# Projecting two attention heads in one matmul: hi and lo halves summed on VectorE, the division by row sums moved ahead of the output projection, reciprocals spread over partitions by two DMAs

## The reference

```python
q, k, v = (split_heads(layernorm(x) @ W) for W in (Wq, Wk, Wv))   # (B, 16, T, 64)
logits = (q @ k.T + causal + pos_bias) / 64
out = softmax(logits) @ v                    # rows divided by their sum
x = x + layernorm(concat_heads(out) @ Wo + bo)
# then shared FFN + 8 experts, top 2 of them weighted, layernorm, residual
```

## Time and profile before

| what | value |
|---|---|
| median of 3 runs | 843.75 us (843.51 to 843.93) |
| the profiled execution's own time | 844.46 us |
| its span, first to last instruction | 842.7 us |
| mean granted TensorE clock | 0.975 |
| TensorE matmuls busy | 771.5 us (92%) |
| VectorE busy | 707.7 us (84%) |
| ScalarE busy | 612.8 us (73%) |
| GpSimd busy | 298.9 us (35%) |

### The profile page before, as it was taken

The page is one execution under the profiler, slowest core; times in us unless marked ns, Lnnn a source line. Parts: engine busy times, 40 slices in busy tenths (PEclk is TensorE's granted clock), DMA queues, the critical chain, the costliest instruction groups (busy, mean ns, idle before and its releaser), DMA issues.

```text
span 842.7 us, 17198 instructions
## 1 busy us (share of the span) xinstructions
PE 771.5 (92%) x4436; PEld 657.1 (78%) x4436; DVE 707.7 (84%) x1596; ACT 612.8 (73%) x1340; POOL 298.9 (35%) x323
## 2 busy tenths in 40 slices
PE   3877999999999999999999999996489999999992
PEld 2656988888888888888889888885377777777771
DVE  5557888988888888888888888888778888898976
ACT  2356888887888888888788888873577767667672
POOL 2318823333332332333233233223503354445423
PEclk9899999999999999999999999999679999999997
DMA  7684334424423432442443343230003211122101
GB/s 279 219 280 89 75 66 97 88 62 87 100 62 76 95 77 62 93 94 62 87 95 67 70 97 82 62 75 26 25 1 129 76 60 43 46 75 75 51 1 50
DMA packets 56025, 70.72 MB, mean 84 GB/s; under 512 B 36032, under 2 KB 45120, under 8 KB 52544
## 3 DMA queue, kind: packets, MB, share of 16 engines
q1 hardware_dynamic: 55712, 69.83, 32.9%
q10 hardware_dynamic: 288, 0.59, 0.3%
HBM read 27.36 MB, written 9.50 MB: 44 GB/s over the span
## 4 chain that ended last, share of the span: by engine, by line
PE 75%; DVE 8%; issue 6%; POOL 4%; ACT 3%; DMA 3%; POOLq 0%; DVEq 0%; ACTq 0%; SPq 0%
PE out_ps L1191 16%; PE score_ps L1158 16%; PE trans_ps L1173 15%; PE shared_ps L1205 6%; PE trans_ps L1074 3%; PE score_ps L1074 3%; PE score_ps L1076 2%; PE score_ps L1075 2%; PE trans_ps L1075 2%; PE trans_ps L1076 2%; DVE pT_lo L961 2%; PE shared_ps L1074 2%; PE shared_ps L1076 2%; PE shared_ps L1075 2%; POOL rstd L421 1%
## 5 line engine op out<-in xcount | busy, mean ns | idle before, releaser
L649 ACT ACTIVATE probs<-score_ps,row_min 128x128 f32<-128x128 f32 (+7 forms) x256 | 189.9, 742 | 53.5 <-DVE row_min L848 53.4
L861 DVE TENSOR_TENSOR pT_lo<-trans_ps,pT_hi 128x512 fp32r<-128x512 f32 (+3 forms) x384 | 201.6, 552 | 16.7 <-ACT pT_hi L670 16.6
L670 ACT ACTIVATE pT_hi<-trans_ps 128x512 fp32r<-128x512 f32 (+3 forms) x384 | 185.1, 491 | 40.4 <-PE trans_ps L1173 28.8
L848 DVE CUSTOM_DVE_ANT_0 score_ps<-score_ps,bias 128x128 f32<-128x128 f32 (+7 forms) x256 | 194.6, 760 | 22.8 <-PE score_ps L1158 19.4
L1173 PE MATMUL trans_ps<-ident,probs 128*128 128x128 f32 x1152 | 190.0, 274 | 3.2 <-DVE pT_lo L861 1.8
L1158 PE MATMUL score_ps<-k_hl,q_hl 128*128 128x512 f32 (+2 forms) x768 | 182.5, 351 | 3.1 <-DMA k_hl<-k_hl 1.6
L470 POOL TENSOR_TENSOR acc<-acc,head_out 128x512 f32<-128x512 f32 x64 | 83.0, 1297 | 245.5 <-DVE head_out L879 245.3
L1173 PEld LDWEIGHTS trans_ps<-ident,probs 128*128 128x128 f32 x1152 | 136.8, 140 | 27.3 <-DVE pT_lo L861 11.9
L1191 PE MATMUL out_ps<-pT_hi,v_hl 128*128 128x512 f32 (+2 forms) x384 | 156.5, 409 | 1.1 <-DVE pT_lo L861 1.1
L961 DVE TENSOR_TENSOR pT_lo<-probs,pT_hi 128x512 fp32r<-128x512 f32 x144 | 133.2, 952 | 25.0 <-ACT pT_hi L728 15.1
L1158 PEld LDWEIGHTS score_ps<-k_hl,q_hl 128*128 128x128 f32 x768 | 134.4, 189 | 23.7 <-DMA k_hl<-k_hl 1.8
(11 more groups left out here) (122 smaller groups left out, 1163.3 us busy)
## 6 DMA issues: line engine op xcount, KB each, us to landing
q_hl<-k_hl SPq DMA_DIRECT2D x64, 256.0 KB, 3.6
k_hl<-k_hl SPq DMA_DIRECT2D x32, 512.0 KB, 4.2
v_scratch<-probs SPq DMA_DIRECT2D x16, 512.0 KB, 4.0
v_raw<-v_scratch SPq DMA_DIRECT2D x32, 256.0 KB, 4.6
bias_all<-gate_scratch SPq DMA_DIRECT2D x8, 1024.0 KB, 4.8
v_raw<-in_Wfc SPq DMA_DIRECT2D x8, 256.0 KB, 4.9
bias<-in_Wproj SPq DMA_DIRECT2D x8, 256.0 KB, 5.3
bias_all<-in_rel_steps SPq DMA_DIRECT2D x1, 1920.0 KB, 12.7
```

What stands on the lines that cost most here:

```text
L649: act.activation(probs[s % 4][:, 0:n], scores_of(s % QB)[:, 0:n], ACT.Exp, bias=row_min[:, s:s + 1], scale=-1.0, accum_out=row_sum[:, s:s ...
L670: act.activation(pT_hi[c][:, CH * g:CH * g + m, q * P:(q + 1) * P], trans_ps[k % 2][:, 0:m * P].rearrange("p (m q) -> p m q", q=P), ACT.Co ...
L848: dve.tensor_tensor_reduce(out=ps, in0=ps, in1=bias_b[b][:, T - n:T], scale=1.0, scalar=3e38, op0=ALU.add, op1=ALU.min, accum_out=row_min[ ...
L861: dve.tensor_tensor(pT_lo[c][dst], trans_ps[k % 2][:, 0:m * P].rearrange("p (m q) -> p m q", q=P), pT_hi[c][dst], ALU.subtract).then_inc(p ...
```

## The change

Heads are taken in pairs. The product with V of an even head is put into partitions 0 to 63 of a tile `o_pair`, that of an odd head into 64 to 127: ScalarE copies the *other* half of `out_ps` across (64 x 512), and VectorE adds the half of `out_ps` that lies in place. When both heads are there, GpSimd multiplies the tile by `inv_all`, the reciprocals of the row sums as rows that are equal over 64 partitions, and one `project_out` per pair (Wo rows of two heads, 128 deep) goes straight into an `add_pair` on VectorE. `Wo2` holds each row once.

The reciprocals lie one per partition (`row_inv`), and are wanted along the free axis. SP carries them: `store_inv` writes 128 x 4 single floats to a DRAM scratch, `load_inv` waits for it to land and reads 512 floats into each of 64 partitions. The reciprocal of rows of part c = 1 is now computed in slot 9 of its batch's eight (slot 1 of the next half-head), that of c = 0 in slot 5. The last pieces of `values` stand in slot 13 instead of 14, so that VectorE's sum can follow in slot 14. The hardware loop's body holds two heads. How q and k are split is the same on both sides. The core of the diff:

```diff
-    PV1 = [11, 11, 11, 12, 13, 13, 14, 14]
-    WO = [11, 15]
+    PV1 = [11, 11, 12, 12, 12, 13, 13, 13]
+    WO = [12, 15]
+    SUM = [10, 14]
+    INV = [5, 9]
+    SUM_SLOT = {QB * b + SUM[c]: (b, c) for b in range(B) for c in range(NC)}
+    INV_SLOT = {QB * b + INV[c]: (b, c) for b in range(B) for c in range(NC)}
...
+    def in_order(engine, iteration):
+        iteration(0, 0, False)
+        with engine.Fori(1, PAIRS) as m:
+            iteration(m * 2 - 1, m, True)
+            iteration(m * 2, m, False)
+        iteration(H - 1, PAIRS, True)
...
+            def store_inv(h, b, c):
+                u = h * (B * NC) + b * NC + c
+                sp.wait_ge(inv_ready, u + 1)
...
+                rows = slice(QB * b + CH * c, QB * b + CH * (c + 1))
+                sp.dma_start(bass.AP(inv_dram.tensor, (b * NC + c) * W, [[1, P], [P, CH]]), row_inv[:, rows],
+                             allow_slow_non_contiguous=True).then_inc(inv_stored, 16)
+            def load_inv(h, b, c, m, odd):
...
+                sp.wait_ge(inv_stored, (h * (B * NC) + b * NC + c) * 16 + 16)
+                sp.dma_start(inv_all[b][c][half_of(odd), :],
+                             bass.AP(inv_dram.tensor, (b * NC + c) * W, [[0, DH], [1, W]])).then_inc(inv_loaded[b][c], 16)
+            def iteration(h, m, odd):
...
                 load_v(h, 1)
+                if not first:
+                    store_inv(h - 1, 1, 1)
+                    load_inv(h - 1, 1, 1, m, not odd)
                 place_q(h, 1)
                 place_k(h, 1)
+                store_inv(h, 0, 0)
+                load_inv(h, 0, 0, m, odd)
                 if not last:
                     sp.wait_ge(v_ready, h * B + 1)
                     load_v(h + 1, 0)
+                store_inv(h, 0, 1)
+                load_inv(h, 0, 1, m, odd)
+                if not last:
                     place_q(h + 1, 0)
                     place_k(h + 1, 0)
+                store_inv(h, 1, 0)
+                load_inv(h, 1, 0, m, odd)
...
-            def add_head(h, b, c):
...
+            def normalise_pair(m, b, c):
+                pool.wait_ge(inv_loaded[b][c], m * 32)
...
+                pool.wait_ge(o_summed, (m * 2 - 1) * (B * NC) + b * NC + c + 1)
...
+                pool.tensor_tensor(o_pair[b][c][:], o_pair[b][c][:], inv_all[b][c][:], ALU.mult).then_inc(o_ready, 1)
...
-                act.activation(oT[c][:], out_ps[:], ACT.Copy).then_inc(oT_ready, 1)
+                act.activation(o_pair[b][c][half_of(odd), :], out_ps[half_of(not odd), :], ACT.Copy).then_inc(o_copied, 1)
...
+            def sum_halves(h, b, c, odd):
+                dve.wait_ge(o_copied, h * (B * NC) + b * NC + c + 1)
+                own_half = o_pair[b][c][half_of(odd), :]
...
+                dve.tensor_tensor(own_half, out_ps[half_of(odd), :], own_half, ALU.add).then_inc(o_summed, 1)
+            def add_pair(m, b, c):
...
+                blocks = acc[:, QB * b + CH * c:QB * b + CH * (c + 1), :]
...
+                dve.tensor_tensor(blocks, shared_ps[:].rearrange("p (t d) -> p t d", d=D), blocks, ALU.add)\
+                   .then_inc(acc_added, 1)
...
-                for slots, do in ((PV_SLOT, invert_sums), (WO_SLOT, scale_head)):
...
+                for n, _, b, c in own_and_carried(INV_SLOT, s, h):
+                    invert_sums(n, b, c)
+                for _, _, b, c in own_and_carried(WO_SLOT, s, h, odd):
+                    add_pair(m, b, c)
...
-                    last = pe.matmul(shared_ps[:, j * P:(j + 1) * P], oT[c][:, j * P:(j + 1) * P],
-                                     wo[:, h, :], start=True, stop=True)
+                    last = pe.matmul(shared_ps[:, j * P:(j + 1) * P], o_pair[b][c][:, j * P:(j + 1) * P],
+                                     wo[:, m - 1, :], start=True, stop=True)
```

More of the change, by code:

```diff
@@ L173, in transformer_block @@
                      for i in range(2)]
-        gated = [head_out[c] for c in range(2)]
+        gated = [o_pair[0][c] for c in range(2)]
         acc_T = acc[:].rearrange("p t d -> p (t d)")
@@ L353, in _ @@
             load_v(0, 0)
-            head(0)
-            with sp.Fori(1, H - 1) as h:
-                head(h)
-            head(H - 1, last=True)
+            in_order(sp, iteration)
+            store_inv(H - 1, 1, 1)
+            load_inv(H - 1, 1, 1, PAIRS, True)
             def load_expert(i, wf, wp):
@@ L524, in _, with iteration @@
             split_v(0, 0)
-            for s in range(S):
-                slot(0, s, False, False)
-            with pool.Fori(1, H - 1) as h:
+            def iteration(h, m, odd):
                 for s in range(S):
-                    slot(h, s, True, False)
-            for s in range(S):
-                slot(H - 1, s, True, True)
+                    slot(h, s, not (isinstance(h, int) and h == 0), isinstance(h, int) and h == H - 1, m, odd)
+            in_order(pool, iteration)
             def split_wfc(e, i):
@@ L685, in slot @@
                     split_hi(h - 1, s - LAG_ACT + S)
-                if s in PV_SLOT:
-                    copy_oT(h, *PV_SLOT[s])
-                if carried and s + S in PV_SLOT:
-                    copy_oT(h - 1, *PV_SLOT[s + S])
+                for n, before, *part in own_and_carried(PV_SLOT, s, h):
+                    copy_other(n, *part, m, odd != before)
                 exp(h, s)
@@ L694, in slot, with iteration @@
                         split_qk_hi(h + nxt, b, half)
-            for s in range(S):
-                slot(0, s, False, False)
-            with act.Fori(1, H - 1) as h:
+            def iteration(h, m, odd):
                 for s in range(S):
-                    slot(h, s, True, False)
-            for s in range(S):
-                slot(H - 1, s, True, True)
+                    slot(h, s, not (isinstance(h, int) and h == 0), isinstance(h, int) and h == H - 1, m, odd)
+            in_order(act, iteration)
             def normalise_moe_in(b):
@@ L884, in slot, with invert_sums @@
-            def slot(h, s, carried, last):
+            def invert_sums(h, b, c):
+                u = h * (B * NC) + b * NC + c
+                rows = slice(QB * b + CH * c, QB * b + CH * (c + 1))
+                if not (isinstance(h, int) and h == 0):
+                    dve.wait_ge(inv_stored, (u - B * NC) * 16 + 16)
+                dve.wait_ge(probs_ready, h * S + QB * b + CH * c + CH)
+                dve.reciprocal(row_inv[:, rows], row_sum[:, rows]).then_inc(inv_ready, 1)
+            def sum_halves(h, b, c, odd):
+                dve.wait_ge(o_copied, h * (B * NC) + b * NC + c + 1)
+                own_half = o_pair[b][c][half_of(odd), :]
+                dve.sem_inc(dve_passed, 1)
+                dve.tensor_tensor(own_half, out_ps[half_of(odd), :], own_half, ALU.add).then_inc(o_summed, 1)
@@ L885, in slot @@
+            def slot(h, s, carried, last, m, odd):
                 row_minimum(h, s)
+                for n, before, b, c in own_and_carried(SUM_SLOT, s, h):
+                    sum_halves(n, b, c, odd != before)
                 if s >= LAG_DVE:
@@ L898, in slot, with iteration @@
                         split_qk_lo(h + nxt, b, half)
-            for s in range(S):
-                slot(0, s, False, False)
-            with dve.Fori(1, H - 1) as h:
+            def iteration(h, m, odd):
                 for s in range(S):
-                    slot(h, s, True, False)
-            for s in range(S):
-                slot(H - 1, s, True, True)
+                    slot(h, s, not (isinstance(h, int) and h == 0), isinstance(h, int) and h == H - 1, m, odd)
+            in_order(dve, iteration)
             def add_normed(b):
@@ L1240, in slot, with iteration @@
                     piece()
+            def iteration(h, m, odd):
+                for s in range(S):
+                    slot(h, s, not (isinstance(h, int) and h == 0), isinstance(h, int) and h == H - 1, m, odd)
             for r in range(2):
                 pe.wait_ge((v_evac_act, v_evac_dve)[r], NB)
-            for s in range(S):
-                slot(0, s, False, False)
-            with pe.Fori(1, H - 1) as h:
-                for s in range(S):
-                    slot(h, s, True, False)
-            for s in range(S):
-                slot(H - 1, s, True, True)
-            carried_uses = sorted(t for t in WO_SLOT if t >= S)
+            in_order(pe, iteration)
             for s in range(S, TAIL):
```

177 lines of the change are left out of this document (87 added, 90 removed).

## The result

The changed kernel takes **1217.36 us** (median of 4 runs, 1214.81 to 1222.05) against 843.8 for the kernel before: 1.443 times as long, interval 1.439 to 1.448. I had forecast 899, in a range of 848 to 945. "Slower" was right, the size far off. The profiled execution has a span of 1220.3 us against 842.7, 377.6 more.

What follows compares the result with a forecast made beforehand. TensorE, busy 92%, was taken as the bound, with late k transfers to take over: 30 steps at 18.1 instead of 16.26 us add 55, the end 0.7, to 844.5, giving 900, or 899 against the median; range 848 to 945.

Steps and rivals of the forecast that it cites:

- some 30: TensorE idle ahead of first scores in attention, put down to the k transfer, some 30 times.
- The sum of 64 x 512: VectorE's sum of halves in attention, bounded by nothing and 0.69 us, taken at 0.66 us.
- GpSimd's product: GpSimd's multiplications, four per pair of heads, in place of four additions of 1.30 us per head.
- the first rival: Late k idles TensorE in the loop and its clock falls: up to 45 us more, 944, or 921; chance 0.22.
- x: Time for SP's store of reciprocals to land in DRAM: taken as 3.3 us, bounds about 2.1 and 4.6.
- the round: First scores over reciprocal, store, load, q and k to next first scores: 18.1 us against 16.26; chance 0.52 at full clock.
- q behind the load: In SP's queue the load's 128 KB go ahead of q: 0.3 us taken, bounds nothing and 1.3.
- a loop body twice as long: The hardware loop's longer body, costed at nothing, as no step showed a wait at its end.
- TensorE's 1.78 us less in light half-heads: Half-heads without projection matmuls have 14.48 us of TensorE work; those holding the pair's projections stay at 16.26.
- hidden transfers, 824: Store and load cost nothing, half-heads without projections fall to 14.9 us: 20 us less, 824; chance 0.16.

Runs made afterwards that it cites:

- run 4: Changed kernel with each stored float in a 512-byte DRAM line of its own, loads reading the input instead, division left out: 976.25 us, 1.157 times.
- run 5: Kernel before with seven small transfers of different shapes behind its result, each waited for, three times over: 904.8 us, timed once.
- run 6: Kernel before with more small transfers behind its result (other float distances, a way through an SBUF row), three times over: 930.8 us, timed once.
- run 1: Changed kernel, whole, with q and k transfers issued by SP ahead of the store and load of reciprocals: 1285.14 us, 1.528 times.
- run 2: Kernel before with only the reciprocals at slots 5 and 9 and the 64 stores and 64 loads added, their data unread: 1215.33 us, 1.441 times.
- run 3: Changed kernel without stores and loads of reciprocals, inv_all filled with a constant, division left out: 984.52 us, 1.164 times.
- run 8: Changed kernel without stores and loads, division left out, with the sum of part c = 0 at the end of slot 9, ahead of split_qk_lo: 920.34 us.
- run 10: Kernel before, whole, with only the two tables of places for products with V and projections set as in the changed kernel: 878.85 us, 1.040 times.
- run 9: Kernel before, whole, with two heads instead of one in every engine's hardware loop body: 864.37 us, 1.024 times.
- run 11: The kernel of run 8, division left out, with add_pair on 8 columns instead of 512: 919.82 us, 1.090 times.
- run 12: The kernel of run 11 with sum_halves on 8 columns as well: 901.20 us, 1.067 times.
- run 7: Changed kernel, whole, reciprocals one slot earlier, stores beside q and k, loads behind k, a semaphore per part, earlier c = 0 sum: 1071.78 us, 1.267 times.

## Why the prediction came out as it did

**Right.** Direction and place: q and k behind a store and a load in SP's queue, TensorE idle ahead of first scores 31 times for k ("some 30"). The sum of 64 x 512 takes 0.69 us (0.66 taken), GpSimd's product 1.28 (1.30). The clock fell, as in the first rival, to a mean of 0.858. By the waits it cost next to nothing in the loop: a slower TensorE makes reciprocals and low parts late, and SP waits 17.1 us in all for those.

**The step that failed first: x.** I took 3.3 us and at most 4.6 for the store to land; it is 9.6 in the median (7.8 to 11.9). My bounds came from runs of 256 and 512 bytes and I scaled by their number. Runs 4 to 6 show that neither number nor length is the price: 512 runs of four bytes land in 1.9 us where each stands 512 bytes from the next. The Trainium skill ("DMA: Bandwidth & Descriptors", section "Anatomy of one DMA — SWDGE (gpsimd) path") has a fixed cost of about 2.0, stated for another issuing path; the 1.9 agrees with it, and the store as written takes 7.6 more. Its section "Specifications" gives a read-modify-write for under 512 bytes; that alone doesn't tell the 1.8 us of run 5 from its 7.9, which differ only in the addresses.

**The step that failed second: one store on the round.** I costed the store between reciprocal and q, and left out that SP waits out another in the same half-head (slot 5's). With x = 9.6 my round gives 18.1 + 6.3 = 24.4. SP's queue in series has two landings: 2 x 9.6 + 9.0 for the rest (28.19 - 19.2) = 28.2. The series overtakes the round where 2x + 9.0 = x + 14.8, at x = 5.8; below that, leaving it out would have cost nothing. That the series sets the step is shown by SP's waits, nearly all for landings, and by run 1, where the store is off the round and the step doesn't fall.

**A third term, smaller.** For q behind the load I took 0.3 us, at most 1.3. From q's issue to k's it is 5.69 us in the median, against 4.19 before: 1.5 more. With the spread store of run 4 it is 4.57, 0.4 more. So most of it goes with the slow store; how, no run shows.

**The sum again.** 29 steps x 11.93 = 346; the start, third q issue at 84.60 instead of 76.26, 8.3; from the last q issue to the end 318.1 instead of 294.9, 23.2, with the last stores and loads in a row. Together 377.5 of the 377.6.

**Costed at nothing, and not nothing.** None of it shows in the 1217, since SP's series is longer (run 2 has none of it and takes 1215), but it does with cheaper transfers (run 4: 976):

| part | us | from |
|---|---|---|
| values wait for VectorE's sum | 64 | run 3 - run 8 |
| places of `values` and projections | 34 | run 10 |
| a body of two heads | 20 | run 9 |
| VectorE's two sums per half-head | 19 | run 11 - run 12 |
| `add_pair` | 1 | run 8 - run 11 |

They make 137 of the 141 us of run 3 (before rounding); that they add so well is arithmetic over different kernels, not shown for each pair. I had named "a loop body twice as long" and set it at nothing because the short body shows no wait at its end, which says nothing on a longer one. I hadn't listed the wait of `values` for `o_summed` at all, though the change moves TensorE's wait for `out_ps` from ScalarE to VectorE by it.

**The gain doesn't come through.** TensorE's 1.78 us less in light half-heads doesn't bring them under the 16.26 of before: 17.2 to 17.3 in run 8, and 16.7 in run 12. The fair measure is run 10, which has the same places and takes 17.37 for every half-head. Against it light ones are shorter, by 0.7 us in run 12, and heavy ones longer by as much (18.0), though there both of VectorE's additions are cut to 8 columns; what makes them longer no run shows. VectorE and ScalarE work nearly as long as before in a light half-head (14.5 and 13.7 us); that their work between slots keeps the step is argued. The rival "hidden transfers, 824" falls: even with no such transfers, in run 3, the kernel takes 984.

Left open: whether it is VectorE's own instructions that are late after the jump in the long body, and a version that stores the reciprocals in 16-byte runs (1.41 us) and reads them back in order. That wasn't tried; by run 3 a faster transfer alone doesn't bring this pairing under the kernel before.

## What to carry to other kernels

A queue that waits for landings one after another is an engine: add up all its waits for a whole step, not only those on the path that was short before. Moving a wait behind something else frees the queue and can close another circle, as in runs 1 and 7. Price a transfer by how its pieces lie in the destination's memory, and where no row has such pieces, keep the upper bound open. When a buffer's release moves from one engine to another, look at what stands ahead of it in the new engine's queue.

## What the runs showed of the hardware

- From issue to next issue, 512 four-byte writes to DRAM take 7.9 to 10.0 us side by side, 3.1 to 4.3 at 8 bytes apart, 2.1 to 2.6 at 32 and 64, 1.8 at 512; 128 writes of 16 bytes side by side 1.4 to 1.7. Read side by side from DRAM, 512 floats take 2.1; into SBUF, 16 bytes apart, 2.0 to 2.1 (runs 5 and 6).
- A row in one SBUF partition takes 6.3 us to spread over 64 partitions, the same bytes from DRAM 2.9 to 4.3, issue to issue (run 6).
- A loop body of two heads instead of one makes the step at each of six jumps back some 3.4 us longer (19.65 against 16.2). In it 26 packets of instructions are loaded from 160 to 550 us, in the short body none (run 9).
- TensorE full at 16.26 us a step went to 17.37 when only the places of its fillers moved (run 10).
